# Attention in two fused layers: softmax sums taken by ScalarE beside the row maxima, and P V of four heads side by side in 32-column parts

## What is computed

```python
# layer 1, for each batch
xn = rms_norm(x, g_norm) * (1 + scale) + shift        # scale, shift = emb @ W_emb + b
q, k, v = heads(xn @ W_qkv);  q = rms_norm(q, g_q);  k = rms_norm(k, g_k)
o = softmax(q @ k.T * 32 ** -0.5) @ v
x1 = o + o @ W_out
# layer 2: latent attention with a causal mask, then experts
y = rmsnorm(x1, ln1_w)
q, k = [q_p, rope(q_r)], [k_p, rope(k_r)]              # 16 + 16 channels for each head
h = x1 + softmax(causal(q @ k.T * 32 ** -0.5)) @ v @ o_w
out = x + h + shared_expert(z) + routed_experts(z)     # z = rmsnorm(h, ln2_w); 2 of 7 for each token
```

## Time and profile before

| what | before |
|---|---|
| median of 3 runs | 1292.03 us (1290.21 to 1296.72) |
| profiled execution, span | 1289.1 us (its device time is not listed apart from the span; the median lies 2.9 us above it) |
| PE busy / PEld busy | 1169.7 us (91%) / 825.7 us (64%) |
| DVE busy | 744.4 us (58%) |
| ACT busy | 572.3 us (44%) |
| POOL busy | 290.7 us (23%) |
| first and last exponential of the steps start at | 88.3 and 963.3 us |

### The profile page before, as it was taken

How to read it: one execution, slowest core, us unless ns; L and a number is a source line. 1 busy time by engine, 2 the same in 40 slices (tenths; PEclk the granted TensorE clock), 3 DMA queues, 4 the chain that set the end, 5 groups by cost and what they waited for, 6 DMA issues and landing times.

```text
span 1289.1 us, 18670 instructions
## 1 busy us (share of the span) xinstructions
PE 1169.7 (91%) x6059; PEld 825.7 (64%) x6059; DVE 744.4 (58%) x1807; ACT 572.3 (44%) x1248; POOL 290.7 (23%) x244
## 2 busy tenths in 40 slices
PE   5979999999999889999999989989999999999970
PEld 5745555665566446557767757766657888888850
DVE  6565675477545856666565575566364774444433
ACT  3324464345443555455465454455264753222210
POOL 1313122100210031001011200200124464555530
PEclk9979999999999999999999999999899999999995
DMA  7064243125311732352284264265357744555559
GB/s 255 33 180 131 65 136 112 50 86 184 99 50 58 225 107 57 99 189 88 88 259 149 86 234 122 84 201 176 86 186 232 262 152 105 109 108 113 115 134 331
DMA packets 88127, 178.42 MB, mean 138 GB/s; under 512 B 12609, under 2 KB 23265, under 8 KB 86497
## 3 DMA queue, kind: packets, MB, share of 16 engines
q1 hardware_dynamic: 79216, 156.90, 37.4%
q0 software_dynamic: 8512, 19.93, 8.2%
q10 hardware_dynamic: 304, 0.40, 0.2%
HBM read 110.86 MB, written 65.27 MB: 137 GB/s over the span
## 4 chain that ended last, share of the span: by engine, by line
PE 77%; DVE 8%; DMA 5%; ACT 4%; issue 3%; SPq 1%; POOL 0%; DVEq 0%; ACTq 0%; POOLq 0%
PE psum L862 14%; PE psum L681 9%; PE psum L682 8%; PE psum L683 8%; PE psum L846 6%; PE psum L825 6%; PE psum L690 4%; PE psum L940 4%; PE psum L942 4%; PE psum L941 4%; PE psum L967 2%; PE psum L969 2%; PE psum L968 2%; PE psum L909 2%; PE psum L772 2%
## 5 line engine op out<-in xcount | busy, mean ns | idle before, releaser
L1174 ACT ACTIVATE probs<-psum 128x512 f32<-128x512 f32 (+3 forms) x512 | 257.3, 517 | 231.5 <-PE psum L849 120.6
L825 PE MATMUL psum<-stack 96*128 96x512 f32 (+3 forms) x512 | 210.2, 416 | 8.6 <-DMA stack<-split_s 4.0
L1583 DVE TENSOR_REDUCE nmax<-psum 128x1 f32<-128x512 f32 x256 | 170.5, 684 | 77.0 <-PE psum L825 73.2
L846 PE MATMUL psum<-stack 97*128 97x512 f32 (+3 forms) x512 | 197.3, 386 | 16.8 <-ACT probs L1174 15.4
L862 PE MATMUL psum<-probs,vals 128*33 128x512 f32 (+3 forms) x1024 | 209.4, 531 | 0.0
L1586 DVE CUSTOM_DVE_ANT_0 psum<-psum,causal 128x128 f32<-128x128 f32 (+3 forms) x256 | 123.0, 501 | 21.0 <-PE psum L825 19.4
L825 PEld LDWEIGHTS psum<-stack 96*128 96x128 f32 x512 | 100.0, 196 | 46.3 <-issue 23.7
L846 PEld LDWEIGHTS psum<-stack 97*128 97x128 f32 x512 | 99.0, 193 | 40.0 <-ACT probs L1174 25.8
L862 PEld LDWEIGHTS psum<-probs,vals 128*33 128x33 f32 x1024 | 49.8, 112 | 99.6 <-issue 65.5
L681 PE MATMUL psum<-w_hi,xh 128*128 128x512 f32 (+1 forms) x256 | 95.4, 373 | 4.2 <-DVEq L1449 2.5
L682 PE MATMUL psum<-w_hi,xl 128*128 128x512 f32 (+1 forms) x256 | 93.6, 366 | 0.0
(11 more groups left out here) (238 smaller groups left out, 2338.0 us busy)
## 6 DMA issues: line engine op xcount, KB each, us to landing
stack<-split_s SPq DMA_DIRECT2D x378, 128.0 KB, 3.0
split_s<-split SPq DMA_DIRECT2D x64, 512.0 KB, 3.0
xt<-in_x_dram SPq DMA_DIRECT2D x4, 1024.0 KB, 5.2
x_s<-yt SPq DMA_DIRECT2D x4, 1024.0 KB, 5.0
xt<-x_s SPq DMA_DIRECT2D x4, 1024.0 KB, 4.8
yt<-in_x_dram SPq DMA_DIRECT2D x4, 1024.0 KB, 5.6
res<-x_s SPq DMA_DIRECT2D x4, 1024.0 KB, 8.2
acc_s<-yt SPq DMA_DIRECT2D x4, 1024.0 KB, 6.0
```

Of the source, the lines that this page charges most:

```text
L825: sq.filled(nc.tensor.matmul(psum[:, sq.bank(M), 0:n], st[:, 0, t * P:(t + 1) * P], st[:, 1, 0:n], start=True, stop=True), M)
L846: last = nc.tensor.matmul(psum[:, bank, lo:S], st[:, 1, t * P:(t + 1) * P], st[:, 0, lo:S], start=True, stop=not masked)
L1174: sk.cleared(nc.scalar.activation(probs[:, M % NX, lo:S], psum[:, sk.bank(M), lo:S], ACT.Exp, scale=SCALE), M)
L1583: sq.cleared(V.tensor_reduce(out, psum[:, sq.bank(M), :], AX.X, ALU.max, negate=True), M)
```

## The change

**ScalarE.** The softmax sums no longer come from a column of ones in P V. Instead `exp_sum(a)` is a second exponential for each step: it reads the bank of `scores` in place, with the negated maximum of each row as its bias (a column of 128 values) and ScalarE's accumulator as its output of interest (`accum_out=sums`), and it is this instruction that frees the `sq` bank. In layer 2 it takes the masked, negated scores that `maximum` wrote back. Maxima and scores carry the factor 32 ** -0.5 beforehand. `pair_out` and `max_rows` are no longer ACT's.

**P V.** V has 32 columns, without the ones. Pairs alternate between the lower and upper 64 partitions of bank 7, and the steps are reordered: a run is four steps, the third or fourth tile of both heads of one pair and the first or second of the next pair. The four products of a run write four 32-column parts. In layer 2 the tiles of a head go 0, 2, 1, 3.

**No turns of the result.** GpSimd splits the maxima in two parts, DVE takes the reciprocal of the sums, and one transpose of 24 rows brings all three to rows. Two rows of maxima go to `stack` (98 rows); the reciprocals are stored to DRAM and spread by two DMAs over 32 partitions for each head (`store_sums`, `spread_sums`). `pair_out` on DVE multiplies the pair's result by them where it stands, with channels on partitions, which is what `out` needs. ACT makes o_hi of a chunk (`chunk_hi`), GpSimd the rest (`chunk_lo`). `back` and `turn_o` are gone.

**Steps.** LEAD is 20 and not 16, `stack` has 5 slots for pairs and not 4, `probs` 7 and not 8, the turn of the maxima stands 6 steps ahead. The table beside the steps is new: `out` stands at m = 8, 9, 11, 12 of the next batch.

```diff
-LEAD = 16
-TURN_AHEAD = 5
+NPAIRS = NB * NPR
+LEAD = 20
+TURN_AHEAD = 6
 LAG = 2
-GROUP = 4
-NX = 2 * GROUP
+NX = 7
+T_ORDER = {1: (0, 1, 2, 3), 2: (0, 2, 1, 3)}
...
-        put((5,), [("back", i, NPR - 1)])
-        put((8,), [("turn_o", i, NC - 1)])
-        put((23, 27, 31, 35) if phase(j) == 1 else (25, 29, 33, 37), each("out", i, NT))
+        put((8, 9, 11, 12), each("out", i, NT))
...
+def run_of(r):
+
+    steps = []
+    for p, place in ((r // 2 - 1, 2 + r % 2), (r // 2, r % 2)):
+        if 0 <= p < NPAIRS:
+            t = T_ORDER[phase(p // NPR)][place]
+            steps += [(p, 2 * (p % NPR) + a, t, place) for a in range(2)]
+    return steps
...
-                nc.tensor.matmul(psum[side:side + VW, o.bank(p), lo:S], vals[k % 2][:, t, h, :], probs[:, M % NX, lo:S],
-                                 start=(t == 0), stop=(t == NT - 1)).then_inc(pv_mm, 1)
+                at_ = HALF * (p % 2) + DH * (h % 2)
+                nc.tensor.matmul(psum[at_:at_ + DH, o.bank(p), lo:S], vals[k % 2][:, t, h, :], probs[:, M % NX, lo:S],
+                                 start=(place == 0), stop=(place == NT - 1)).then_inc(pv_mm, 1)
...
+            def exp_sum(a):
+                p, h, t = max_step(a)
+                act.wait_ge(max_ok, a + 1)
+                if p >= 2 and a % STEPS_P == 0:
+                    act.wait_ge(div_ok, p - 1)
+                c = h % 2 * NT + t
+                n, scale = ((t + 1) * P, -1.0) if phase(p // NPR) == 2 else (S, 1.0)
+                x = psum[:, sq.bank(a), 0:n]
+                sq.cleared(nc.scalar.activation(x, x, ACT.Exp, bias=nmax[:, p % 2, c:c + 1], scale=scale,
+                                                accum_out=sums[:, p % 2, c:c + 1]), a)
+
+            def chunk_hi(n):
+                for p in (2 * n, 2 * n + 1):
+                    o.wait_read(act, p)
+                copy(oh[:, n % NC, :], od[:, n % NC, :]).then_inc(o_hi, 1)
...
-                sk.cleared(nc.scalar.activation(probs[:, M % NX, lo:S], psum[:, sk.bank(M), lo:S], ACT.Exp, scale=SCALE), M)
-                if pair_done(M) is not None:
-                    pair_out(pair_done(M))
-                if max_turn(M) is not None:
-                    max_rows(max_turn(M))
+                p, h, t, place = STEPS[M]
+                lo = t * P if phase(p // NPR) == 2 else 0
+                sk.cleared(nc.scalar.activation(probs[:, M % NX, lo:S], psum[:, sk.bank(M), lo:S], ACT.Exp), M)
+                if M + LEAD - 1 < NSTEPS:
+                    exp_sum(M + LEAD - 1)
+                if M in CHUNK_AT:
+                    chunk_hi(CHUNK_AT[M])
...
+            def chunk_lo(n):
+                pool.wait_ge(o_hi, n + 1)
+                nc.gpsimd.tensor_tensor(ol[:, n % NC, :], od[:, n % NC, :], oh[:, n % NC, :].bitcast(F32),
+                                        ALU.subtract).then_inc(o_lo, 1)
...
+            def pair_out(p):
+                at_, c = pair_at(p)
+                dve.wait_ge(pv_mm, LAST_STEP[p] + 1)
+                dve.wait_ge(rb_ld[p % 2], 32 * (p // 2 + 1))
+                if p == 0:
+                    dve.wait_ge(spare_set, 3 * 16)
+                if p % NPR == 0 and p:
+                    ring.wait_full(dve, ("out", p // NPR - 1, NT - 1))
+                o.cleared(V.tensor_tensor(od[at_, c, :], psum[at_, o.bank(p), :], rb[at_, :], ALU.mult), p)
```

More of the change, by code:

```diff
@@ L104, in beside_heads @@
         for g in range(NG):
-            late = 3 if k == 0 and g == 0 else 0
-            put((28, 29) if g == 0 and k else (33, 34) if g == 0 else (30 + 8 * g, 31 + 8 * g), hscales(j, g))
-            put((32 + 8 * g + late, 34 + 8 * g + late), turns(j, g))
+            put((base - 3 + 4 * g, base - 2 + 4 * g), hscales(j, g))
+            turns(j, g, base + 4 * g)
     elif j < NB:
-        put((2, 5), [("kv_d", j), ("q_d", j)])
-        for n in range(2 * NT):
-            put((9 + 2 * n, 10 + 2 * n), [("qk", j, n), ("rope", j, n)])
@@ L124, in beside_heads @@
             put((31, 35, 36, 39), scale)
-        put((60, 61, 62, 63), each("x", after, NC))
-    put(range(13, 64, STEPS_P), each("back", k, NPR - 1))
-    put((38, 46, 57), each("turn_o", k, NC - 1))
+            put((60, 61, 62, 63) if k > B else (56, 57, 58, 59), each("x", after, NC))
     if k == 0:
@@ L326, in build @@
         probs = rest("probs", [P, NX, S])
-        vals = [rest(f"vals{n}", [P, NT, H, VW]) for n in range(2)]
+        vals = [rest(f"vals{n}", [P, NT, H, DH]) for n in range(2)]
         vs = rest("vs", [P, 2, S])
@@ L782, in beside @@
                     if t == 0:
-                        for c in (NC - 2, NC - 1):
-                            ring.wait_read(pe, ("turn_o", j, c))
+                        pe.wait_ge(o_lo, NC * (j + 1))
                         if j == 0:
@@ L989, in _ @@
             tile_turn(1)
-            beside(("back", LAST, NPR - 1))
             gate_up(0, 0)
-            beside(("turn_o", LAST, NC - 1))
             gate_up(0, 1)
@@ L1024, in _, with copy @@
         def _(act):
-            def copy(out, src):
-                return nc.scalar.activation(out, src, ACT.Copy)
+            def copy(out, src, scale=1.0):
+                return nc.scalar.activation(out, src, ACT.Copy, scale=scale)
             def bank_of(key):
@@ L1183, in _ @@
                         beside(key)
-            pair_out(NB * NPR - 1)
+            for M in CHUNK_AT:
+                if M >= NSTEPS:
+                    chunk_hi(CHUNK_AT[M])
             def split_expert(e, c):
@@ L1345, in _ @@
                             beside(key)
+            for M in CHUNK_AT:
+                if M >= NSTEPS:
+                    chunk_lo(CHUNK_AT[M])
             for t in range(NT):
@@ new lines, in divide, with maxima_step @@
+            def divide(p):
+                for n in range(STEPS_P - 3, STEPS_P):
+                    sq.wait_read(dve, STEPS_P * p + n)
+                if p >= 2:
+                    ring.wait_full(dve, ("max", p - 2))
+                V.reciprocal(rr[:, p % 2, 2 * STEPS_P:], sums[:, p % 2, :]).then_inc(div_ok, 1)
+            def maxima_step(a):
+                if a < NSTEPS:
+                    maximum(a)
+                if a in DIVIDE_BEHIND:
+                    divide(DIVIDE_BEHIND[a])
@@ L1776, in split_expert @@
                                 erh[:, e, 2 * c:2 * c + 2, :].bitcast(F32), ALU.subtract).then_inc(er_lo2, 1)
+            for M in OUT_AT:
+                if M >= NSTEPS:
+                    pair_out(OUT_AT[M])
             lo_of_x(0)
-            beside(("back", LAST, NPR - 1))
             lo_of_x(1)
-            beside(("turn_o", LAST, NC - 1))
             hidden(0)
```

379 lines of the change are left out of this document (204 added, 175 removed).

## The result

The changed kernel took 1357.0 us (median; 1356.0 to 1362.1) beside 1292.5 us for the kernel before in the same session: ratio 1.0496, 95% interval 1.0466 to 1.0525. It is some 64 us slower, where 1264 and "faster" were forecast and the range ended at 1309. The profiled execution has a span of 1354.9 us.

What follows compares the result with a forecast made beforehand. The prediction took PE to be full in the steps, and level with ACT after the change. Steps -42, start +6 and the wait of `out` +8 gave -28 us: 1264 us, range 1212 to 1309.

Steps and rivals of the forecast that it cites:

- Level engines do not add up to their larger sum: Steps: PE and ACT, now level, are summed by stretches, the larger counting; 33 to 48 us less, 42 taken.
- the factor 1.085: Steps: measured 877 us over the 808 summed before, for waits the sum leaves out; carried over to the changed kernel.
- sum of stretches of eight steps: Steps: the larger of PE's and ACT's time in each eight steps, over all batches; 808 us before, 778 after.
- the wait of `out`: Output products: PE stands about 2 us once a batch for POOL's rest; 8 us in all (0 to 16).
- the start: Before the first step: 20 scores pass PE, DVE and ACT through three banks; 6 us more, first exponential about 94.
- PE's saving: PE in the steps: P V in four parts, `back` and `turn_o` gone; some 140 us, 131 after group starts.
- ACT's term: ACT in the steps: `exp_sum` at 0.70 us in layer 1, 0.53 in layer 2; 315 us more, some 48 leaving.
- four parts run as two: Rival on P V: PE keeps 90 us of its 140 and leads again; 1315 us, chance 0.05.
- dear bias or dear accumulator: Rival on ACT: each `exp_sum` takes 0.1 us more than priced, 0.80 for 512 columns; 1309 us, chance 0.17.
- The waits eat it: Rival: `out` waits 3 us or more each batch and its chain lies on ACT's full queue; 1285 us, chance 0.12.
- The engines fit together: Rival: the table spaces work so well that sixteen or more steps are the right stretch; middle 1217 us, chance 0.16.
- three signs of being wrong: `exp_sum` dearer than 0.76 us, four parts not running together, or layer 2's batches gaining as much as layer 1's.

Runs made afterwards that it cites:

- e1: Changed kernel without `exp_sum`: DVE frees the score bank, sums are ones and the division by them is left out; 1259.5 us.
- f4: Changed kernel without `exp_sum` (DVE frees the bank, sums are ones) and with the output products three steps later; 1247.1 us.
- e2: Kernel before with `exp_sum` alone added, its sums unused, freeing the score bank in place of DVE; 1376.1 us.
- g1: Changed kernel with layer 1's `exp_sum` at full width but off the banks, layer 2's left out, DVE freeing the banks; 1301.6 us.
- f3: Changed kernel with the turned score ahead of the untransposed one in PE's step; 1343.2 us.
- h3: Kernel before with the turned score ahead of the untransposed one in PE's step; 1294.2 us.
- i2: Changed kernel with each `exp_sum` one step earlier on ACT, still behind the exponential; 1381.6 us.
- g2: Changed kernel with two banks for the untransposed scores instead of three; 1777.1 us.
- f2: Changed kernel with ten spare matmuls in front of each of the seven waits of the output products; 1357.2 us.
- h1: Kernel before with each of the 512 untransposed score products done twice; 1344.4 us.
- g4: Changed kernel without `exp_sum`, with output products three steps later and each untransposed score product done twice; 1275.3 us.
- e4: Changed kernel with each untransposed score matmul issued twice into the same bank; 1383.8 us.

## Why the prediction was wrong

**The step that failed** is "Level engines do not add up to their larger sum": it took PE's work in the steps down by 131 us at full worth, and it carried the factor 1.085 for the waits from the kernel before to one in which a third engine stands in the banks' cycle. By its own sum of stretches of eight steps, 778 us, the factor measured is 930/778 = 1.195, with both errors in it. The steps were to be 34 us shorter, with the wait of `out`, and are 55 longer. Of the rest, the start holds (+7 instead of +6), and the experts' +4 was not foreseen.

**PE's saving was mis-sized.** The group of four P V at 1.0 and 0.55 was right at the full clock: the medians over the steps are 1.00 and 0.57. The means are 1.19 (groups that begin with 512 columns), 1.21 (384) and 0.64 (128): 28 of 127 groups ran below the full clock, where it was 6 of 128 before. So P V lost 63 us of work, not 90. `back` and `turn_o` were priced at 51 us by the lengths of their rows; by distances they kept PE for 32 (L772 20, `o_chunk` 13). The scores and the products, whose matmuls are as many and as wide as before, took 24 and 13 us more than before, at the lower clock and with waits of weight loads that count as work. The sum has a slip as well: 0.15 us for the start of each group takes the 141 us to 131 only for 64 groups, and there are 128, so the price should have been 122. 131 became 36, and in e1, where the clock is the same 0.92, 63.

**What the saving is worth.** The 63 us are of all of PE's work. By the runs above they are worth 43 to 55 in the schedule of before (0.7 to 0.9), and 26 to 30 in the new table (0.4 to 0.5); e1 gained 31 to 33 against before, with the start 3 us later. So the new table takes back part of what PE saves. Of its own waits, the output products' is worth 12 us without `exp_sum` (f4). What ACT's waits for the store of `split` cost in all (24 us in e1, 9.4 in the changed kernel) was not tried apart. Their largest in the changed kernel shows in its timelines of PE, ACT and SP's queue:

```profile
700.10 0.22 PE L873 MATMUL psum<-mask,identr 128*128 128x128 f32 x1
707.16 0.48 PE L850 MATMUL psum<-stack 96*128 96x128 f32 x1 [6.84 <-ACT psum L1141]
```

```profile
699.39 0.20 ACT L1141 ACTIVATION_READ_ACCUMULATOR psum<-psum,nmax 128x1 f32 x1
705.57 0.60 ACT L1051 ACTIVATE split<-psum 128x512 fp32r<-128x512 f32 x1 [5.97 <-DMA split_s<-split]
```

```profile
695.39 0.43 SPq L640 DMA_DIRECT2D wo_raw<-in_L_ffn_o_w_dram  x1
...
696.73 0.34 SPq L498 DMA_DIRECT2D split_s<-split  x1
```

PE's row says that it waits for `exp_sum`; ACT's says why there is none: it stands 5.97 us for the store of `split` (L498), which was issued 1.3 us behind the load of the 1 MB of `wo_raw` and landed 8.8 us after its issue, where the median of these stores is 3.3. The prediction put the DMAs that the change adds at nothing. This store is not one of them: both kernels have it, and the closer spacing of the turned items brought it into ACT's way, which no term covered.

**ACT's term.** `exp_sum` costs 97 us in the changed kernel (e1) and 84 in the kernel before (e2). Its own duration was priced well (0.66 against 0.70). The prediction saw its cost in the steps as load alone, and nearly half is not: in layer 1 25 of 55 us go when `exp_sum` keeps its time on ACT but DVE frees the banks (g1). That the banks' cycle is on the path is also what f3 beside h3, i2 and g2 show. The prediction read "three banks" only for the start.

**The rivals.** No rival gave the time: 1315 ("four parts run as two") and 1309 ("dear bias or dear accumulator") come nearest, and the mechanisms of both are refuted, by the group of 1.00 us and by an `exp_sum` at my price and not 0.1 above it. "The waits eat it" named the wait of `out` (it was 2.1 us, seven times, as forecast) and not the one that ate the gain. "The engines fit together" fell.

What a column operand costs can be read from g1, where the spare exponential has one and writes to SBUF, as do the squares of the same run, which have an accumulator too and no column (behind the bar: busy us, mean ns of one):

```profile
L1148 ACT ACTIVATE junk<-causal,gqk 128x512 f32<-128x512 f32 x256 | 186.7, 729 | 6.6 <-DVE nmax L1636 4.2 <-ACT junk L1148 0.7
...
L1078 ACT ACTIVATE junk<-xt 128x512 f32<-128x512 f32 x32 | 20.3, 633 | 1.6
```

729 less 633 is 96 ns, with Exp in the one and Square in the other. The Trainium skill's page "ScalarE: Activation LUTs", section "What ACT_TABLE_LOAD costs", puts a column operand at about 93 ns, and this trace agrees. `exp_sum` itself reads and writes PSUM and is 0.67 us long (median), so the column did not make it dearer than 0.70.

**What would have shown it.** Right: the group of 1.0, `exp_sum` with its read, the first exponential at 95.3, `out` at 2.1 us a batch, PE's waits for ACT above 60 us. Wrong: ACT's share (71%, not over 75%), since the steps were longer; PE's (85%, not 80%), since its work fell by 36 us and not by 131; and layer 1, which was to get some 35 us shorter and got 34 longer, while layer 2, with "little" to gain, lost 20. Of the three signs of being wrong, a dear `exp_sum` and parts that do not run together did not turn up; the third did, though not as it was meant: layer 2 lost less than layer 1. None of them watched the waits for a bank. What the kernel before could have told and was not asked: PE idled only 53 us in its steps, with DVE alone between it and a free bank; the added turn of each bank (0.66 us for 512 columns, 512 times) was set against ACT's time and against nothing else.

**What stays open.** How the 97 us of `exp_sum` divide in layer 2; what the spacing of the turned items is worth by itself; whether a fourth bank would take the waits away; and how much of the loss is the lower clock and how much the standing that goes with it, since no run changed one without the other (f2 left both as they were).

## What to carry to other kernels

When a step puts one more engine between a buffer's filling and its freeing, count the buffers against that engine's order before counting its time: here three banks were enough for PE and DVE, and with ACT behind them, their hold cost layer 1 nearly as much (25 us) as ACT's work itself (30). Before taking a saving on the busiest engine at full worth, double one of its small instructions in a run: here that showed 0.6 before and 0.3 after. And where a wait names an engine that is not full, look at that engine's own timeline: the 6.8 us that PE waited for `exp_sum` were ACT's wait for a store.

## What the runs showed of the hardware that was not expected

Four fp32 products in four 32-column parts take 1.06 us for 512 columns where two and two take 1.91, so the array runs all four at once. And the granted clock goes with how PE's work is spaced. The timeline of the changed kernel's PE at the start of batch k = 1 shows two short waits and, behind them, rows of one product of twelve matmuls:

```profile
232.57 0.49 PE L850 MATMUL psum<-stack 96*128 96x512 f32 x1 [0.90 <-ACT psum L1141]
...
233.72 0.50 PE L850 MATMUL psum<-stack 96*128 96x512 f32 x1 [0.32 <-ACT psum L1141]
...
236.76 0.63 PE L722 MATMUL psum<-w_lo,xh 128*128 128x512 f32 x1
237.18 0.63 PE L720 MATMUL psum<-w_hi,xh 128*128 128x512 f32 x1
237.61 0.63 PE L721 MATMUL psum<-w_hi,xl 128*128 128x512 f32 x1
...
238.42 0.39 PE L720 MATMUL psum<-w_hi,xh 128*128 128x512 f32 x1
238.66 0.40 PE L721 MATMUL psum<-w_hi,xl 128*128 128x512 f32 x1
```

At 236.76 to 237.61 the starts are 0.42 and 0.43 us apart, the lower level (1.2 GHz, granted clock 0.50 from 236.7 to 238.1); from 238.42 on they are 0.24 apart, the upper one (2.4 GHz, granted clock 1.00), with the same instructions and no wait between. Over the steps the granted clock was 0.99 in h1 (PE idle 28 us), 0.98 before (53), 0.97 and 0.95 in g4 and f4 (54 and 84), 0.92 in the changed kernel (143) and 0.73 with two banks (344). The sum of idle time does not set it alone: e4 and f3 idle 105 and 106 us, at 0.95 and 0.91. No run separates the clock from the standing, but it is one way in which added work may cost less than its size and saved work bring less.
